# Weighting expert rows at their copy out of PSUM and adding them to the residual by the gathering DMA

## What is computed

```python
x = x + xattn0(norm(x), ctx)     # cross attention, self attention, gelu FFN
x = x + moe(norm(x))             # the part that the change touches
x = x + xattn1(norm(x), ctx)     # cross attention, 16 heads of 16
x = x + mod(norm(x))             # 128 of 256 tokens of a block go through an FFN

def moe(h):                      # 8 "experts", the last of them is a no-op; top 2; capacity 256
    w = softmax(h @ router_w.T + router_b)
    mask = top2(w) > 0
    # expert e takes the first 256 tokens whose mask holds e
    out_e = relu(h[tok_e] @ w_in[e]) @ w_out[e] * w[tok_e, e]
    return scatter_add(out_e) + h * (w[:, 7] * mask[:, 7])
```

## Time and profile before

| what | value |
|---|---|
| median of 3 runs | 890.43 us (881.79 to 892.51) |
| profiled execution, span from first to last instruction | 873.5 us |
| mean granted TensorE clock | 0.927 |
| PE / DVE / ACT / POOL busy | 731.3 / 643.2 / 464.0 / 414.4 us |
| instructions on DVE / POOL | 1244 / 394 |
| bytes moved by DMA | 81.49 MB |
| HBM read / written | 36.74 / 10.11 MB |

### The profile page before, as it was taken

One profiled execution on the slowest core, in us unless ns is written; L12 is line 12 of the kernel. 1 busy time (PEld: TensorE's weight loads), 2 busy tenths in 40 slices (PEclk: granted clock), 3 DMA queues, 4 the chain that ended last, 5 costly groups with the idle time before them and its releaser, 6 DMA issues.

```text
span 873.5 us, 18486 instructions
## 1 busy us (share of the span) xinstructions
PE 731.3 (84%) x7282; PEld 611.0 (70%) x7282; DVE 643.2 (74%) x1244; ACT 464.0 (53%) x739; POOL 414.4 (47%) x394
## 2 busy tenths in 40 slices
PE   5678999999999778999962799953589799779996
PEld 4556777777777547999852799953457577548996
DVE  7657988888888654798986386743977888766863
ACT  4246767777777566574512254410155557665451
POOL 9755564534664464536457231127674263543200
PEclk9879999999999899999985799995679999999998
DMA  6776787679775603001030676444677656400101
GB/s 189 124 125 114 135 125 104 97 121 139 112 116 99 75 3 98 25 2 38 20 115 11 209 263 209 141 89 80 100 124 106 86 85 94 56 2 2 37 25 37
DMA packets 57066, 81.49 MB, mean 93 GB/s; under 512 B 8434, under 2 KB 35057, under 8 KB 56932
## 3 DMA queue, kind: packets, MB, share of 16 engines
q1 hardware_dynamic: 53730, 74.11, 44.2%
q0 software_dynamic: 3072, 6.04, 3.1%
q10 hardware_dynamic: 178, 0.16, 0.1%
HBM read 36.74 MB, written 10.11 MB: 54 GB/s over the span
## 4 chain that ended last, share of the span: by engine, by line
PE 61%; DVE 20%; issue 5%; POOL 5%; ACT 4%; DMA 3%; SPq 1%; POOLq 0%; DVEq 0%; ACTq 0%
PE ps L209 12%; PE ps L211 10%; PE ps L210 10%; PE ps L740 7%; DVE nmax L1515 7%; PE ps L808 7%; PE ps L762 5%; PE ps L961 3%; POOL moe_in L1357 3%; ACT prob L1073 2%; DMA kst<-k_parts 2%; PE ps L782 1%; PE ps L242 1%; PE ps L233 1%; SPq L527 1%
## 5 line engine op out<-in xcount | busy, mean ns | idle before, releaser
L1515 DVE TENSOR_REDUCE nmax<-ps 128x4 f32<-128x1024 f32 x192 | 234.4, 1223 | 71.9 <-PE ps L740 70.4
L1073 ACT ACTIVATE prob<-ps 128x1024 f32<-128x1024 f32 x192 | 196.4, 1023 | 72.4 <-PE ps L762 70.2
L1282 POOL TENSOR_TENSOR rstd<-var,half 128x2 f32<-128x2 f32 x56 | 44.9, 802 | 249.4 <-DVE var L1449 176.5
L740 PE MATMUL ps<-kst,qst 50*128 50x256 f32 (+1 forms) x768 | 99.2, 340 | 35.0 <-DVE nmax L1515 28.4
L740 PEld LDWEIGHTS ps<-kst,qst 50*128 50x128 f32 (+1 forms) x768 | 61.2, 197 | 66.6 <-DVE nmax L1515 45.3
L808 PE MATMUL ps<-prob,vext 128*32 128x256 f32 x1536 | 104.5, 390 | 0.6 <-ACT oext L1086 0.6
L762 PE MATMUL ps<-qst,kst 51*128 51x256 f32 (+1 forms) x768 | 83.2, 295 | 15.6 <-ACT prob L1073 12.7
L762 PEld LDWEIGHTS ps<-qst,kst 51*128 51x128 f32 (+1 forms) x768 | 61.3, 193 | 22.9 <-ACT prob L1073 16.4
L808 PEld LDWEIGHTS ps<-prob,vext 128*32 128x32 f32 x1536 | 40.6, 110 | 31.0 <-issue 1.8
L1290 POOL TENSOR_SCALAR hres<-xres,mv,rstd 128x256 f32<-128x256 f32 x48 | 60.6, 1269 | 2.5
L1086 ACT ACTIVATE oext<-ps 128x256 f32<-128x256 f32 x96 | 36.9, 385 | 28.1 <-PE ps L782 15.7
(11 more groups left out here) (277 smaller groups left out, 2330.5 us busy)
## 6 DMA issues: line engine op xcount, KB each, us to landing
kst<-k_parts SPq DMA_DIRECT2D x138, 128.0 KB, 5.6
qst<-q_parts SPq DMA_DIRECT2D x132, 128.0 KB, 4.0
e_raw<-in_ein SPq DMA_DIRECT2D x7, 1024.0 KB, 5.3
e_raw<-in_eout SPq DMA_DIRECT2D x7, 1024.0 KB, 6.0
ctx_raw<-in_ctxT SPq DMA_DIRECT2D x16, 256.0 KB, 5.7
out<-xres SPq DMA_DIRECT2D x8, 256.0 KB, 2.1
moe_in<-zeros SPq DMA_DIRECT2D x14, 128.0 KB
moe_out<-vext SPq DMA_DIRECT2D x7, 256.0 KB, 5.9
```

The source lines that it names most:

```text
L740: last = pe.matmul(score_pair(n, p)[:, 512 * s + S * t:512 * s + S * (t + 1)], qst[j][a:b, p, t * P:(t + 1) * P], kst[j][a:b, p, :], start ...
L1073: act.activation(probs[p % 4][:].rearrange("p i t s -> p (i t s)"), T_PS, ACT.Exp).then_inc(sm["exp_done"], 1)
L1282: last = gp.tensor_tensor(rstd[i][:], var[i][:], half[:], ALU.pow)
L1515: dve.tensor_reduce(nmax[n % 2][:, :, :, p].rearrange("p t s -> p s t"), score_pair(n, p).rearrange("p (s t k) -> p s t k", s=2, t=TB), AX ...
```

## The change

The weight of a row is applied when the expert's result leaves PSUM, and the gathering DMA adds the row to `xres`.

- `hres` and `moe_in` get eight more columns: the eight expert weights of the token travel with its row. ScalarE's exponential of the router writes them there directly, and `route` normalizes them in place. `hb(n)` is cut to the first 256 columns.
- The padding columns of `moe_in` are zeroed by one more DMA of SyncE, behind the zero row of `moe_out`.
- Behind the token load of expert 1, SyncE loads `yw`, the weights of all slots.
- The copy out of PSUM (L1674) becomes two multiplications by the slot's weight.
- `gat`, `wsel`, `combine` and the last step of `route` go. `add_rows(b, r)` issues two indirect DMAs with `compute_op=add` whose destination is `xres`. The two ranks of one block never run together: rank 1 waits for rank 0's semaphore, and rank 0 of the next block is issued ahead of that wait (`b` = 0) or behind rank 1 (`b` >= 1).
- Item `16 + b` waits for the DMAs of block `b` in place of `combine(b)`.
- In `POOL_ORDER` gathers 6 and 7 change places; the entries of `DVE_ORDER` for `combine` go.

```diff
-    moe_in = nc.dram_tensor("moe_in", [NE * CAP, D], F32, kind="Internal").ap()
+    moe_in = nc.dram_tensor("moe_in", [NE * CAP, D + 8], F32, kind="Internal").ap()
...
-        hres = sb("hres", [P, NT, D])
+        hres = sb("hres", [P, NT, D + 8])
...
-            "attention 16.1": "attention 19.0", "gather 7.0": "attention 18.1", "gather 6.0": "context 12.0",
+            "attention 16.1": "attention 19.0", "gather 6.0": "attention 18.1", "gather 7.0": "context 12.0",
...
                     sp.dma_start(moe_out[NE * CAP:NE * CAP + 1, :], zeros[0:1, :]).then_inc(sm["zero_out"], 16)
+                    sp.dma_start(moe_in[:, D:D + 8].rearrange("(i p) c -> p i c", p=P),
+                                 zeros[:, 0:8 * NE * TB].rearrange("p (i c) -> p i c", c=8)).then_inc(sm["zero_out"], 16)
...
+                    if e == 1:
+                        sp.dma_start(yw[:], moe_in[:, D:D + NE].rearrange("(i p) c -> p i c", p=P)).then_inc(sm["yw_ld"], 16)
...
+                def add_rows(b, r):
+                    for t in range(TB):
+                        tile = TB * b + t
+                        gp.indirect_dma_start(xres[:, tile, :], None, moe_out, bass.IndirectOffsetOnAxis(ap=slu[:, tile, r:r + 1], axis=0),
+                                              bounds_check=NE * CAP, oob_is_err=True, compute_op=ALU.add).then_inc(sm[f"gat_ld{b % 4}"], 16)
+
                 def gather(b):
...
                     if b == 0:
+                        gp.wait_ge(sm["keep_s"], B)
                         gp.wait_ge(sm["st_y0"], 16 * 4)
                         gp.wait_ge(sm["st_y1"], 16 * 3)
-                    if b >= 4:
-                        gp.wait_ge(sm["comb_s"], b - 3)
-                    for t in range(TB):
-                        for r in range(2):
-                            gp.indirect_dma_start(gat[:, b % 4, t, r, :], None, moe_out, bass.IndirectOffsetOnAxis(ap=slu[:, TB * b + t, r:r + 1], axis=0),
-                                                  bounds_check=NE * CAP, oob_is_err=False).then_inc(sm[f"gat_ld{b % 4}"], 16)
+                        add_rows(0, 0)
+                    if b + 1 < B and b < 1:
+                        add_rows(b + 1, 0)
+                    gp.wait_ge(sm[f"gat_ld{b % 4}"], 64 * (b // 4) + 32)
+                    add_rows(b, 1)
+                    if b + 1 < B and b >= 1:
+                        add_rows(b + 1, 0)
...
                         if layer(n) == SECOND:
-                            dve.wait_ge(sm["comb_s"], n - NA + 1)
+                            dve.wait_ge(sm[f"gat_ld{n % 4}"], 64 * ((n - NA) // 4 + 1))
...
-                    yield route_at(g, 6)
-                    ch(dve.tensor_tensor(part, pick, wts.unsqueeze(2).to_broadcast(sh3), ALU.mult))
-                    ch(dve.tensor_reduce(wsel[:, a:b, :], part, AX.X, ALU.add))
...
-                    dve.tensor_copy(YE[e % 2], e_out(e)).then_inc(sm["y_ready"], 1)
+                    if e == 0:
+                        dve.wait_ge(sm["yw_ld"], 16)
+                    for t in range(TB):
+                        last = dve.tensor_scalar(YE[e % 2][:, t * D:(t + 1) * D], e_out(e)[:, t * D:(t + 1) * D], yw[:, TB * e + t, e:e + 1], None, ALU.mult)
+                    last.then_inc(sm["y_ready"], 1)
...
-                def combine(b):
-                    yield start_of(NA + b) - 23.4
-                    dve.wait_ge(sm[f"gat_ld{b % 4}"], 64 * (b // 4 + 1))
-                    for r in range(2):
...
-                        for t in range(TB):
-                            tile = TB * b + t
-                            last = dve.scalar_tensor_tensor(xres[:, tile, :], gat[:, b % 4, t, r, :], wsel[:, tile, r:r + 1], xres[:, tile, :], ALU.mult, ALU.add)
```

More of the change, by code:

```diff
@@ L260, in hb @@
         def hb(n):
-            return hres[:, TB * (n % B):TB * (n % B) + TB, :]
+            return hres[:, TB * (n % B):TB * (n % B) + TB, 0:D]
         def xb(n):
@@ L422, in mod_start @@
             return T_M0 + M_STEP * i
-        RT = dict(wts=0, rank=128, rmask=256, tmp=384, valid=512, slotx=640, gt=768, eq=1024, pick=1280, part=1344)
+        RT = dict(rank=128, rmask=256, tmp=384, valid=512, slotx=640, gt=768, eq=1024, pick=1280, part=1344)
         SP_ORDER = {
@@ L1547, in attention @@
                     else:
-                        dve.tensor_tensor(flat(res[:]), G[2], flat(hb(n)), ALU.add).then_inc(sm["res_s"], 1)
+                        dve.tensor_tensor(res[:], by_tile(G[2]), hb(n), ALU.add).then_inc(sm["res_s"], 1)
                         yield t0 + later(n, 26.6)
@@ L1570, in ffn @@
                         dve.wait_ge(sm["h_ready"], NA)
-                    dve.tensor_tensor(flat(res[:]), PV_PS, flat(hb(f)), ALU.add).then_inc(sm["fres_s"], 1)
+                    dve.tensor_tensor(res[:], by_tile(PV_PS), hb(f), ALU.add).then_inc(sm["fres_s"], 1)
                     dve.wait_ge(sm["fres_s"], f + 1)
@@ L1609, in by_rank @@
                         return rt[:, at:at + 16 * nt].rearrange("p (t r e) -> p t r e", r=2, e=8)
-                    wts, rank, rmask, tmp, valid, slotx = (field(k) for k in ("wts", "rank", "rmask", "tmp", "valid", "slotx"))
+                    rank, rmask, tmp, valid, slotx = (field(k) for k in ("rank", "rmask", "tmp", "valid", "slotx"))
+                    wts = hres[:, a:b, D:D + 8]
                     gt, eq, pick, part = square("gt"), square("eq"), by_rank("pick"), by_rank("part")
@@ L1681, in keep @@
                     for t in range(TB * b, TB * b + TB):
-                        last = dve.scalar_tensor_tensor(xres[:, t, :], hres[:, t, :], noop[:, t:t + 1], xres[:, t, :], ALU.mult, ALU.add)
-                    ch(last)
-                def combine(b):
-                    yield start_of(NA + b) - 23.4
-                    dve.wait_ge(sm[f"gat_ld{b % 4}"], 64 * (b // 4 + 1))
-                    for r in range(2):
-                        if r:
-                            yield start_of(NA + b) - 22.4
-                            dve.wait_ge(sm["comb_a"], b + 1)
-                        for t in range(TB):
-                            tile = TB * b + t
-                            last = dve.scalar_tensor_tensor(xres[:, tile, :], gat[:, b % 4, t, r, :], wsel[:, tile, r:r + 1], xres[:, tile, :], ALU.mult, ALU.add)
-                        last.then_inc(sm["comb_a" if r == 0 else "comb_s"], 1)
+                        last = dve.scalar_tensor_tensor(xres[:, t, :], hres[:, t, 0:D], noop[:, t:t + 1], xres[:, t, :], ALU.mult, ALU.add)
+                    last.then_inc(sm["keep_s"], 1)
                 def mod(i):
@@ L1736, in _ @@
                              *(attention(n) for n in ITEMS), *(ffn(f) for f in range(B)), *(route(g) for g in range(len(GROUPS))),
-                             *(expert(e) for e in range(NE)), *(expert_weights(e) for e in range(NE)), *(keep(b) for b in range(B)), *(combine(b) for b in range(B)), *(mod(i) for i in range(B)))
+                             *(expert(e) for e in range(NE)), *(expert_weights(e) for e in range(NE)), *(keep(b) for b in range(B)), *(mod(i) for i in range(B)))
 def kernel(**inputs):
```

21 lines of the change are left out of this document (10 added, 11 removed), and 10 rows, old and new, of the table DVE_ORDER.

## The result

| | before | after |
|---|---|---|
| median of 20 runs each | 887.17 us (878.53 to 894.64) | 898.62 us (889.62 to 905.01) |
| profiled execution: span | 873.5 us | 893.6 us |
| mean granted TensorE clock in it | 0.927 | 0.913 |

What follows compares the result with a forecast made beforehand. The prediction took the chain as 61% TensorE, 20% VectorE, 3% DMA. Its terms summed to +1.2 us, a span of 874.7 in place of 873.5; with 16.9 carried over, 891.6 us, range 880 to 910.

Steps and rivals of the forecast that it cites:

- rival (B): Accumulating DMA is dear and GpSimd becomes the bound: at 2.0 us an issue +21, 911.6 us; chance 0.12.
- the prediction's own sign: Forecast wrong if the stretch 583 to 700 us changed by over 5 us, or another stage moved over 3 us.
- I take the gather's cost, since it moves the same 1 KB rows: Third layer's start: an accumulating DMA priced like a gather, 1.0 us an issue, plus 0.3 us for the extra landing.
- The start: Third layer's start: ten issues and two waits ahead of GpSimd's `rstd` in place of eight issues; +2.5 us.
- 620 us: Two pieces of removed `xres` additions leave the chain and nothing takes their place; −1.8 us.
- 639 us: Ahead of item 19's transposes, a 2.3 us stall from GpSimd's queue replaces 2.4 us of VectorE additions; net +0.8 us.
- 684 and 690 us: Removed `xres` additions leave the chain where VectorE leads and GpSimd has slack; −2.7 us.
- Weighted copy +0.2, wider rows +0.2: Expert stage: two multiplications replace each PSUM copy, +0.2 us; rows of 1056 B in place of 1024 B, +0.2 us.
- The small store: At 210 us, the padding store of 1792 pieces of 32 B on SyncE's queue delays `m_hi`; +2.0 us.
- Rival (C): The small store holds `m_hi` at 0.115 us a piece, 11.9 us in place of 2.0: 901.5 us; chance 0.10.
- The last step: From profiled span to median: the median stood 16.9 us above the span, and this was carried over, giving 891.6 us.
- Rival (A): VectorE pays in full: waits find data landed, small store hides, all 6.9 us go; 884.0 us; chance 0.28.

Runs made afterwards that it cites:

- experiment 1: The changed kernel with its 32 accumulating DMAs made plain gathers overwriting `xres` (also `oob_is_err=False`), order and waits kept; ratio 0.9991 to the kernel before.
- experiment 2: The changed kernel with rank 1 rows added to `hres` in place of `xres` and no waits between ranks; ratio 1.0022 to the kernel before.
- experiment 12: Blocks 6 and 7 by accumulating DMA, blocks 0 to 5 by plain gathers and VectorE additions, rows carrying weights; ratio 0.9955 to the kernel before.
- Experiment 3: The changed kernel with plain gathers to `gat` and plain VectorE additions in the old order; carried weights and small store stay; ratio 1.003 to before.
- experiment 7: The changed kernel with blocks 0 and 1 gathered plainly and added on VectorE, blocks 2 to 7 accumulated in another GpSimd order; ratio 1.0059 to before.
- experiment 8: The kernel before, with only its fifth gather moved behind item 19's `rstd` and `hres` on GpSimd; ratio 1.0128 to the kernel before.

## Why the prediction came out as it did

The time, 898.62, lies in the range given, and the change made no difference of 2%, the likeliest of the three classes. The mechanism of the forecast was not the one that acted. What acted is rival (B), the dear accumulating DMA, which had a chance of 0.12, together with the waits between the ranks: neither alone costs the 1.3% (experiments 1 and 2). That the time is in the range is luck as far as the mechanism goes: the range was wide enough to hold most of (B). By the prediction's own sign, a stretch from 583 to 700 us more than 5 us longer, the forecast was wrong: `rstd` of item 21 comes 91.6 us behind the cast and came 75.0 before.

- **The step that failed** is "I take the gather's cost, since it moves the same 1 KB rows". An issue measured 1.55 us, not 1.00. The bytes are the same and the packets are not: 96 more for each DMA. The rule of the Trainium skill ("Collectives: The Full Stack", Part 3), quoted with rival (B), that an add needs two source reads and two read descriptors, pointed this way; the packets and the issue time point the same way, by more than from two to three, though no run here shows what GpSimd writes, or whether `oob_is_err=True` has a part in it. The argument against it, that an issue takes 1.0 us whatever its direction, was drawn from copies alone and says nothing about an addition.
- **The start: +2.5 forecast, +5.8 measured.** The queue was read rightly: at gather's prices it gave `rstd` 15.9 us behind the cast, and experiment 1, the same queue at those prices, measured 16.2. The landing that ends the second wait took 6.32 us where 6.3 was assumed. With accumulation it is 19.6, 3.4 us more: ten issues at 0.55 us, less 1.8 by which the second wait shrank (3.10 to 1.26) and the part of `rstd` that overlaps the last issue.
- **620 us: −1.8 forecast.** The additions are gone from the chain, but VectorE was not what ended the stretch any more: the chain from 585 to 659 us goes through GpSimd and its landings. Not paid.
- **639 us: +0.8 forecast.** The mechanism, a wait of GpSimd turned into a stall ahead of item 19's transposes, was right in place and releaser; the stall was 15.76 us, not 2.3. From the end of the preceding `hres` to the end of the last issue ahead of `rstd` of item 19 I had 13.3 us and the trace has 23.6 (632.0 to 655.6). The difference, 10.3, is: 2.7 for the first wait, which I had called free; 3.7 for the issues, some 1.87 us apart and not 1.30; 3.1 for a landing of 7.29 us in place of the 4.2 of the earlier trace rows; 0.7 from that landing to the next issue. The landing of one gather of before was taken for that under other traffic.
- **684 and 690 us: −2.7 forecast.** Not to be seen in the change, which was behind by then; real in experiment 12, where GpSimd keeps its time ahead of these blocks.
- **Weighted copy +0.2, wider rows +0.2.** The expert stage moved by −0.3 us. Experiment 3 bounds all of it at +0.7%.
- **The small store: +2.0 forecast, 0.3 measured.** `yw` with its 1792 pieces of 28 B landed in 3.7 us. Rival (C) and the estimate of 0.037 us a piece are both too high. The rule of the Trainium skill ("DMA: Bandwidth & Descriptors", Specifications) on transfers under 512 B, quoted in the prediction, would have put the stall near its upper end; the trace shows nothing of the size.
- **The last step**, span to median: the 16.9 us were run to run variation. The predicted median, 891.6, was 4.4 above the median of before over 20 runs, which is +0.5% where +1.3% was measured.
- **Rival (B)'s own price** was +6 us at 1.5 us an issue; the medians give +11.4. It had 4.2 us for the landing ahead of item 19 where 7.29 were measured. Rival (A) did not occur: VectorE's saving is real (16.4 us), and did not pay with GpSimd's queue as it stood.

## What to carry to other kernels

A DMA that adds is not priced like one that copies (1.55 us an issue here against 1.00): measure its issue on the engine that issues it, and multiply by the issues that stand ahead of the work someone waits for, not by all of them. An order between two DMAs (rank 1 behind rank 0) becomes a wait in an in-order queue, and its price is a landing under that stretch's traffic, which can be more than what one row shows (7.29 us here against 4.2); put other work between the two. Move work off the engine that leads only in those stretches where the engine that takes it has slack: here that was two blocks of eight. And change the flags of an instruction one at a time, or the experiment can't say which of them costs.

## What the runs showed of the hardware

- An indirect DMA of 128 rows of 1 KB held GpSimd 1.00 us as a gather and 1.55 us with accumulation (median of 32, from 1.547 to 1.687), with the same 0.30 us between two of them, and had 96 packets more. The accumulating ones also had `oob_is_err=True`, the plain ones not; the two were never separated.
- The small work directly behind an accumulating issue was recorded longer: `rstd` at 1.27 us, starting within the issue's record (605.66 + 1.55 is past 606.71), and at 0.73 us behind plain ones in experiment 1. The records overlap by about that difference, so it is no extra time.
- Landings in the stretch of the stacked queries and keys: 3.8 us at least and up to 7.9 in the change, 9.62 for a row addition (experiment 7) and 10.27 for a plain gather (experiment 8). Over all 32 the medians of before and after are the same, 4.2 us (2.8 to 7.6 before). At the second wait of the start the landing took 6.32 us in the change and 6.31 with plain gathers (experiment 1); ahead of item 19 it took 7.29 and 5.34, at other neighbouring traffic. So a long landing needs no addition; whether an addition lengthens one in the busy stretch stays open.
- 1792 stores of 32 B ahead of a small store that TensorE needs made TensorE wait 0.32 us (up to 0.51 in other traces); with the stores cut up the wait is gone, and the timed runs show no difference.
